# First attention of a three-layer block: the softmax weights turned by VectorE in 32x32 blocks and moved by 16 SBUF transfers per half batch, instead of transposed on TensorE

## The reference, cut to what matters

```python
x = x + xattn(layernorm(x), ctx, ctx, mask, w_q, w_k, w_v, w_o)   # 16 batches, 64 queries, 1601 keys, 16 heads of 32
x = x + attn(layernorm(x), w_qkv, ..., w_proj)                    # self-attention over 64 tokens, LoRA on q and v
x = x + ffn(layernorm(x), wg1, wg2, We, be)                       # 20 experts of 512x512, the two best per token

# xattn: the part that is changed
key, value = proj(ctx, w_k), proj(ctx, w_v)
scores = einsum('bhqd,bhkd->bhqk', query, key) / sqrt(32)
scores = where(mask == 0, -1e9, scores)
attn = softmax(scores, -1)
out = einsum('bhqk,bhkd->bhqd', attn, value)
```

## Time and profile before

| | us |
|---|---|
| median of three runs | 772.93 |
| profiled execution, first to last instruction | 772.6 |
| TensorE busy (matmul) | 708.0 |
| VectorE busy | 410.2 |
| ScalarE busy | 360.6 |
| GpSimd busy | 289.0 |

### The profile page before, as it was taken

How to read it: one execution, slowest core, us unless ns; L and a number is a source line. 1 busy time by engine, 2 the same in 40 slices (tenths; PEclk the granted TensorE clock), 3 DMA queues, 4 the chain that set the end, 5 groups by cost and what they waited for, 6 DMA issues and landing times.

```text
span 772.6 us, 16928 instructions
## 1 busy us (share of the span) xinstructions
PE 708.0 (92%) x6817; PEld 581.6 (75%) x6817; DVE 410.2 (53%) x938; ACT 360.6 (47%) x665; POOL 289.0 (37%) x259
## 2 busy tenths in 40 slices
PE   1999999999999999999999999999999766999970
PEld 0787788778878887888788977887778554788860
DVE  5834434453344424533543345735368348799965
ACT  2425445453545345535454343533455431599950
POOL 0005135513553255225532453432225132788530
PEclk9999999999999999999999999999999985799995
DMA  8401101220021101110110002021001580999818
GB/s 294 149 1 43 45 2 45 98 91 24 29 98 44 44 2 44 44 39 7 44 44 2 3 3 75 1 79 45 3 29 57 188 303 21 330 394 397 333 52 326
DMA packets 30268, 74.77 MB, mean 97 GB/s; under 512 B 4053, under 2 KB 4437, under 8 KB 29155
## 3 DMA queue, kind: packets, MB, share of 16 engines
q1 hardware_dynamic: 25778, 65.16, 23.6%
q0 software_dynamic: 4400, 8.41, 2.9%
HBM read 66.13 MB, written 13.44 MB: 103 GB/s over the span
## 4 chain that ended last, share of the span: by engine, by line
PE 86%; DVE 6%; DMA 3%; ACT 2%; issue 2%; SPq 0%; POOL 0%; DVEq 0%; POOLq 0%; ACTq 0%
PE bank L188 22%; PE bank L190 21%; PE bank L189 20%; PE bank L194 10%; PE bank L345 4%; PE bank L322 3%; DMA raw<-in_wq 2%; DVE x_sb L1611 1%; PE bank L564 1%; DMA wr<-scratch_ys 1%; PE bank L551 1%; PE bank L665 1%; PE bank L580 1%; DVE wh L1084 1%; DVE stats L1340 0%
## 5 line engine op out<-in xcount | busy, mean ns | idle before, releaser
L1637 POOL TENSOR_SCALAR pp<-pp,rl 128x400 f32<-128x400 f32 x128 | 163.8, 1297 | 234.8 <-DVE rl L1162 234.8
L1217 DVE COPY pt<-bank 128x512 f32<-128x512 f32 x64 | 44.3, 692 | 99.4 <-PE bank L194 99.3
L188 PE MATMUL bank<-chi,wk 128*128 128x400 f32 x256 | 93.5, 365 | 0.0
L844 ACT ACTIVATE pp<-pp,acc 128x400 f32<-128x400 f32 x128 | 79.0, 619 | 28.0 <-DVE acc L1250 27.7
L1250 DVE CUSTOM_DVE_ANT_0 pp<-bank,cap 128x400 f32<-128x400 f32 x128 | 66.8, 569 | 46.5 <-PE bank L322 46.5
L190 PE MATMUL bank<-chi,wk 128*128 128x400 f32 x256 | 88.3, 345 | 0.0
L189 PE MATMUL bank<-clo,wk 128*128 128x400 f32 x256 | 88.3, 345 | 0.0
L188 PE MATMUL bank<-wv,chi 128*128 128x512 f32 x200 | 83.5, 417 | 0.0
L189 PE MATMUL bank<-wv,chi 128*128 128x512 f32 x200 | 78.5, 393 | 0.0
L190 PE MATMUL bank<-wv,clo 128*128 128x512 f32 x200 | 78.5, 392 | 0.0
L761 ACT ACTIVATE pt<-bank 128x512 f32<-128x512 f32 x64 | 38.2, 597 | 76.4 <-PE bank L194 75.3
(11 more groups left out here) (238 smaller groups left out, 1387.4 us busy)
## 6 DMA issues: line engine op xcount, KB each, us to landing
wr<-in_We SPq DMA_DIRECT2D x13, 1024.0 KB, 11.6
craw<-in_ctx SPq DMA_DIRECT2D x16, 800.0 KB, 4.4
raw<-in_We SPq DMA_DIRECT2D x8, 1024.0 KB, 10.5
acc<-in_We SPq DMA_DIRECT2D x6, 1024.0 KB, 11.0
scratch_xn<-acc SPq DMA_DIRECT2D x16, 256.0 KB
wr<-scratch_ys SPq DMA_DIRECT2D x8, 512.0 KB, 7.2
x_sb<-in_x SPq DMA_DIRECT2D x2, 1024.0 KB, 8.5
out_dram<-x_sb SPq DMA_DIRECT2D x8, 256.0 KB, 5.9
```

Source lines behind the costliest of these rows:

```text
L188: pe.matmul(o, lhs[0], rhs[0], start=start, stop=False)
L844: act.activation(frame(p8), frame(p8), ACT.Exp, bias=bias, scale=-1.0, accum_out=total).then_inc(S["a_exp"], 1)
L1217: dve.tensor_copy(pt[:, p8 % 4, :, :].rearrange("p a c -> p (a c)"), at("t", 8 * (n - 1) + p8)[:, :]).then_inc(S["v_pt"], 1)
L1637: pool.tensor_scalar(frame(p8), frame(p8), rl[:, n % 2, p8:p8 + 1], None, ALU.mult).then_inc(S["g_pn"], 1)
```

## The change

The turns leave TensorE. VectorE transposes each 32x32 block of a tile in place in its grid (`turn`), into `square`, a buffer for each half of a batch that lies in the two `raw` tiles. Blocks then have to change their quarter of the partitions: `shuffle` on SyncE issues, for each half batch, 16 transfers from SBUF to SBUF, one for each pair of a source quarter and a target quarter, each of 32 partitions by 4 rows of 512 bytes (64 KB), into `pt`, which has two halves now. `pv_part` waits for all 16.

The sums of the products move to bank 3 and no longer share banks with the scores, so `s_part` no longer waits for `o_first`, and keys, values and early projections go round three banks in place of four. The lists of all engines are written anew. `wo` is loaded and split in step 0; `w2q` and `w2k` are loaded after the loop, since `square` lies in `raw`. `oh` holds two tiles in place of four.

```diff
+        turned, spreads = [banks[:, 3, 256 * j:256 * j + 256].rearrange("p (g q) -> p g q", g=4) for j in range(2)]
-        pt = sb("pt", [128, 4, 4, 128], f32, second)
+        pt = sb("pt", [128, 2, 4, 4, 128], f32, second)
+        square = [raw[:, 1 - h].rearrange("p k n -> p (k n)").rearrange("p (b x) -> p b x", b=16) for h in range(2)]
             def pv_part(n, half):
-                pe.wait_ge(S["v_pt"], 4 * n + 2 * half + 2)
-                pe.wait_ge(S["a_pt"], 4 * n + 2 * half + 2)
+                pe.wait_ge(d_sh[half], 256 * (n + 1))
...
             def cross(seg):                                  # TensorE
+                for n in range(16 * seg, 16 * seg + NB):
+                    old = n > 16 * seg
+                    values = list(range(made(n), made(n + 1)))
+                    if n:
+                        for g in range(3):
+                            k_part(n, g)
+                    s_part(n, 0)
+                    if old:
+                        pv_part(n - 1, 0)
+                    if n:
+                        k_part(n, 3)
+                    v_part(n, values[0])
+                    s_part(n, 1)
+                    if old:
+                        pv_part(n - 1, 1)
+                    for j in values[1:]:
+                        v_part(n, j)
+                last = 16 * seg + NB - 1
+                for half in range(2):
+                    if not seg:
+                        early_out(2 * half)
+                        early_out(2 * half + 1)
+                    pv_part(last, half)
...
             def cross(seg):                                  # ScalarE, per step
+                    if n:
+                        k_part(n, 0)
+                    if n + 1 < 16 * seg + NB:
+                        context(n + 1)
+                    if n:
+                        k_part(n, 2)
+                    if n == 0:
+                        act.wait_ge(S["p_q"], 8)
+                        weight_hi(wh[0], raw[:, 0], (d_raw[0], 48))
+                    exps(n, seg, 0)
+                    exps(n, seg, 1)
+                    value(n, values[0])
+                    exps(n, seg, 2)
+                    value(n, values[1])
+                    exps(n, seg, 3)
+                    for j in values[2:]:
+                        value(n, j)
...
+            def turn(n, p8):                                 # VectorE
+                half, j = divmod(p8, 4)
+                dve.wait_ge(S["g_pn"], 8 * n + p8 + 1)
+                if n and j == 0:
+                    dve.wait_ge(d_sh[half], 256 * n)
+                c = D * p8 + PW - CW * (n % 8) % 128
+                dve.transpose(square[half][:, :, 32 * j:32 * j + 32],
+                              pp[:, c:c + 512].rearrange("p (b x) -> p b x", b=16)).then_inc(S["v_pt"], 1)
...
+                for n in range(first, last + 1):
+                    old = n > first
+                    if old:
+                        for p8 in (5, 6, 7):
+                            turn(n - 1, p8)
+                    if n < last:
+                        context(n + 1)
+                    if n:
+                        k_part(n, 1)
+                    if n == 0:
+                        weight_lo(wh[0], raw[:, 0], 4)
+                    maxima(n, seg, 0)
+                    maxima(n, seg, 1)
+                    share(n, 0, seg)
+                    if n:
+                        k_part(n, 3)
+                    share(n, 1, seg)
+                    turn(n, 0)
+                    turn(n, 1)
...
+                    elif old:
+                        o_first(n - 1)
+                    maxima(n, seg, 2)
+                    maxima(n, seg, 3)
+                    share(n, 2, seg)
+                    turn(n, 2)
                     share(n, 3, seg)
+                    turn(n, 3)
+                    turn(n, 4)
...
+            def shuffle(n, half):                            # SyncE
+                sp.wait_ge(S["v_pt"], 8 * n + 4 * half + 4)
+                if n:
+                    sp.wait_ge(S["p_pv"], 2 * n - 1 + half)
+                of = square[half].rearrange("p (i a) x -> p a i x", a=4)
+                for a in range(4):
+                    for to in range(4):
+                        sp.dma_start(pt[32 * to:32 * to + 32, half, :, a, :],
+                                     of[32 * a:32 * a + 32, to]).then_inc(d_sh[half], 16)
...
+                context(first + 1, 1, chunk)
+                if seg == 0:
+                    sp.wait_ge(S["v_w"], 3)
+                    sp.dma_start(raw[:, 0], t["wo"]).then_inc(d_raw[0], 16)
+                for n in range(first, last + 1):
+                    if n > first:
+                        shuffle(n - 1, 1)
+                    if n + 2 <= last:
+                        context(n + 2, n + 2 - first, chunk)
+                    shuffle(n, 0)
+                shuffle(last, 1)
+                sp.wait_ge(d_sh[0], 256 * (last + 1))
...
+            sp.dma_start(raw[:, 1], t["w2q"]).then_inc(d_raw[1], 16)
             sp.drain().then_inc(S["s_bar"], 1)
             sp.wait_ge(S["s_bar"], BARRIER)
 
+            sp.dma_start(raw[:, 0], t["w2k"]).then_inc(d_raw[0], 16)
```

More of the change, by code:

```diff
@@ L229, in perceiver @@
         uses = [("q", m) for m in range(4)] + [("k", g) for g in range(4)] + [("q", 4 + m) for m in range(4)]
[L230 to L241, removed]
+        for n in range(16 * NC_):
+            uses += [("k", 4 * n + g) for g in range(4) if n] + [("v", j) for j in range(made(n), made(n + 1))]
+            if n == NB - 1:
+                uses += [("e", i) for i in range(EARLY)]
         use_of = {use: n for n, use in enumerate(uses)}
         def read_by(what, i):
-            if what == "t":
-                return S["a_pt" if i % 2 else "v_pt"], i // 2 + 1
             if what == "k":
@@ L252, in at, with early @@
         def at(what, i):
[L253 removed]
+            return pb[use_of[what, i] % 3]
         def freed(what, i):
             n = use_of[what, i]
[L258 removed]
+            return [read_by(*uses[n - 3])] if n >= 3 else []
+        def early(v, i):
+            return v[:, :, i % 2 * 128:(i % 2 + 1) * 128]
         def tensor(pe):
@@ L379, in redo @@
                     pe.wait_ge(S["s_redo"], REDONE + 4 * i + 2)
-                    out_product(i, oh, at("e", i)).then_inc(S["s_redo"], 1)
+                    out_product(i).then_inc(S["s_redo"], 1)
                 pe.wait_ge(S["s_redo"], REDONE + 4 * EARLY)
             def cross(seg):
[L384 to L390, removed]
-                        pv_part(n - 1, 0)
-                        for p8 in range(4, 8):
-                            t_part(n - 1, p8)
-                        early_out(2)
-                        pv_part(n - 1, 1)
[L396 to L405, removed]
@@ L415, in tensor @@
+                if seg:
+                    spread(last)
             turn_x(0)
@@ L802, in cross @@
             def cross(seg):
-                for n in range(16 * seg, 16 * seg + NB + 1):
-                    old, new = n > 16 * seg, n < 16 * seg + NB
-                    if n and not old:
+                for n in range(16 * seg, 16 * seg + NB):
+                    values = list(range(made(n), made(n + 1)))
+                    if seg and n == 16 * seg:
                         context(n)
[L807 to L818, removed]
+                    if n:
+                        k_part(n, 0)
@@ L836, in cross @@
[L836 to L849, removed]
@@ L850, in cross @@
-                    value(made(n) + 2)
-                    value(made(n) + 3)
-                    if not seg and 0 <= n - SPLIT < EARLY:
+                    exps(n, seg, 0)
[6 more added lines that the diff above has]
+                        value(n, j)
+                    if not seg and 0 <= n - SPLIT < 2:
@@ L1227, in cross @@
                     if old and seg:
-                        o_more(n - 1, b - 1)
+                        o_more(n - 1, n - 1 - first)
                     elif old:
                         o_first(n - 1)
-                    if n == NB and not seg:
-                        dve.wait_ge(S["p_o"], 4)
-                        early_add(3).then_inc(S["v_x1"], 1)
-                    if not new:
-                        break
-                    if n == 4:
-                        weight_lo(wh[0], raw[:, 0], 4)
@@ L1261, in cross @@
-                    share(n, 3, seg)
+                    maxima(n, seg, 2)
+                    maxima(n, seg, 3)
+                    share(n, 2, seg)
+                    turn(n, 2)
+                    share(n, 3, seg)
+                    turn(n, 3)
+                    turn(n, 4)
+                    if not seg and 0 <= n - 1 - SPLIT < 2:
+                        dve.wait_ge(S["a_h"], n - SPLIT)
+                        early_lo(n - 1 - SPLIT).then_inc(S["v_h"], 1)
+                for p8 in (5, 6, 7):
+                    turn(last, p8)
@@ new lines, in cross @@
+                if not seg:
```

(12 more changed lines are left out.)

152 lines of the change are left out of this document (59 added, 93 removed).

## The result

The kernel after takes 876.2 us (870.4 to 878.2, five runs) where the kernel before takes 773.0: ratio 1.131, interval 1.128 to 1.135. It is slower by 13%, outside the range that was forecast and on the other side.

The account below looks back on a forecast made before the run. TensorE's list bounded the kernel before; after, the step P is the longest of that list (21.46 us) and two loops through the transfers, 23.2 us. The sum 398.7 + 15 P gave 747 us, range 726 to 790.

Parts of the forecast that it names:

- What bounds the kernel, and what is removed: TensorE's list bounds the loop; removing four groups of transposes saves 3.6 us a step, from 25.06 to 21.46 us.
- loop B: Path through SyncE's queue that closes at pv_part(n, 1): 6.9 + 31 d + 2.3 = 23.15 us a step.
- tail: Stretch from the start of pv_part(n-1, 1) to the last turn of half 0, turn(n, 3): 6.9 us.
- landing: Time of a transfer from issue to arrival: 2.3 us, with ends 0.45 and 4.4.
- rival 3: DMA engines pace the train at 0.71 us a transfer: step 31.2 us, kernel 867 us; chance 0.09.
- Issue: Spacing of consecutive transfer issues on SyncE's queue: 0.45 us, with ends 0.36 and 0.55.
- d: Time between two consecutive issues in SyncE's queue, taken as 0.45 us; 0.01 us of it is 4.7 us of the kernel.
- Rival 2: SyncE's issue becomes the bound, slower beyond break-even 0.506 us; at 0.55 a step of 26.3, kernel 793 us; chance 0.22.
- Beginning: Step 0, from the first scores at 62.06 to pv_part(0, 0): 22.7 us.
- End: After pv_part(15, 0): 8.9 us to the last copy, then weight_lora some 4 us later, with 1.0 put in the sum.
- VectorE's turns: In-place transposes on VectorE: 0.69 us each, with ends 0.42 and 1.38; eight a step add 5.5 us.
- The three banks and the load of the context: Three banks in place of four cost nothing; the context load's 4.4 us, between SyncE's two trains, are hidden.

Follow-up runs that it names:

- experiment 4: The changed kernel with one transfer per half batch in place of 16 from the second batch on (output not right): 738.2 us, ratio 0.953 against the kernel before.
- experiment 1: A kernel without the attention, issuing only trains of 16 transfers of one shape; the shape of the change cost 0.65 us an issue on SyncE.

## Why the prediction was wrong, step by step

**What bounds the kernel, and what is removed.** Right. TensorE's own list was to fall to 21.46 us a step; experiment 4 has 21.57 on average with three value tiles, 3.6 less than before.

**The loop through SyncE.** The mechanism was right, in place and in kind: loop B, `pv_part(n, 1)` to `pv_part(n + 1, 1)` through 32 issues in one queue. Its tail was forecast at 6.9 us and is 6.73 at full clock. The landing was 2.3 and is 2.1, and doesn't grow; rival 3 (engines pace the train) is wrong.

**The step that failed** is the term *Issue*: "I take d = 0.45, with the ends 0.36 (just under the cheapest train) and 0.55 (just over the dearest)." It measured 0.674 (20.9 us for 31), outside both ends. With it B is 6.9 + 20.9 + 2.3 = 30.1 us where I had 23.15, and the sum 398.7 + 15 x 30.1 = 850 us: 104 us of the 122 between the forecast and the profiled span of 868.4. One reason is experiment 1's answer: I had written that none of the rows is a transfer inside SBUF, and then took bounds from the cheapest and the dearest of them all the same, as if size and rows were what varied. All of those I read for d were simple loads. The other is a misreading: 0.55 was not over the dearest. The same trace of before has this pair of loads in SyncE's queue, 0.60 each by the division that gave 0.39 and 0.51:

```profile
2.13 1.20 SPq L1762 DMA_DIRECT2D qc<-in_rows  x2
```

With 0.60 as the upper end B is 27.8 us and the kernel 816, still short of the result but clearly slower. Rival 2 had the mechanism, the break-even at d = 0.506 and the side; with d = 0.55 for its price, its 793 us are 83 too low.

**The remaining 18 us.** *TensorE's clock*: I had no term for it. After some of the waits `pv_part` takes 1.93 instead of 1.10 us, and keys stand 0.33 apart (280.05 to 280.38) instead of 0.18: the granted clock, 0.89 over a step, has fallen to the lower of its two levels there. Where this comes behind `pv_part(n, 1)`, it is in the tail. So it is here, one step ahead of the one shown above:

```profile
226.64 1.94 PE L332 MATMUL bank<-pt,vv 128*32 128x64 f32 x64 [2.60 <-DMA pt<-raw]
228.51 0.80 PE L191 MATMUL bank<-wv,chi 128*128 128x512 f32 x1
229.10 0.63 PE L192 MATMUL bank<-wv,chi 128*128 128x512 f32 x1
229.53 0.63 PE L193 MATMUL bank<-wv,clo 128*128 128x512 f32 x1
```

```profile
236.18 21.55 SPq L1802 DMA_DIRECT2D pt<-raw  x32
```

Products of the value tile stand 0.43 apart, not 0.23; it is 9.54 us to the first issue and 32.6 to the next `pv_part(n, 1)`, against 6.73 and 29.8 in the step behind it. Over all 15 steps the mean is 30.88, 1.1 us a step above the step at full clock, 17 in all, from which the landing and the tail, each 0.2 shorter than in the formula, take 5 back. *Beginning*: `pv_part(0, 0)` stands at 88.56, 3.8 us later than 62.06 + 22.7; 2.1 of them go to the lower clock behind TensorE's wait of 5.1 us for the maxima (granted clock 0.50 from 68.14 to 72.30), and 1.5 are its wait for the first train, which takes 3.5 us more than 16 x 0.45 and was to be hidden. *End*, 18.1 us from `pv_part(15, 0)` to `weight_lora` for 8.9 + 4.0: 10.4 in place of 7.2 to the second half's `pv_part`, the train again, and 7.7 in place of 5.7 from there, with 6.6 us of waiting for `w2q`. What follows took 2.6 less than before.

**VectorE's turns** were 0.69 by the nearest row and are 0.684. The three banks and the load of the context cost nothing visible, as forecast.

**The chances.** One hundredth of a us of d was 4.7 us of the kernel, as the text said. A quantity with that lever, measured on no row of its kind, deserved a far wider range than 0.36 to 0.55. The cheap fix was also in plain sight: the sum had one queue with 32 issues, while GpSimd was busy for 10.15 us of 25.

## What to carry over

Before a kernel moves a tile by many small transfers, count the issues per step and queue, and price each at what a transfer of just that kind costs to issue; bytes and rows come after that. If the train is longer than its cover, split it over a second queue with idle time before anything else is changed: here this alone turned 1.131 into 0.958. A bound taken from rows of another kind (loads, for copies inside SBUF) isn't a bound, and when the result hangs on it, the range must say so.

## What the runs showed of the hardware that was not expected

- An issue on SyncE cost 0.63 to 0.66 us for all shapes within SBUF and for four rows out of HBM, 16 to 256 KB; a contiguous row of 2 KB per partition out of HBM 0.46; on GpSimd 0.55, and the same in the full kernel, behind its multiplications and with VectorE at work (8.68 us for 16).
- What an issue takes also depends on what stands ahead of it in the queue. The load of the context took 0.33 us to issue in the kernel before, each of the 15 times (line 1777), with an idle queue, and 0.59 right behind a train in the kernel after (287.53); after a pause of 0.34 us it took 0.33 again (348.07). A single issue read after a pause is no price for a train.
- The Trainium skill, in "DMA: Bandwidth & Descriptors", section "Bandwidth", gives 0.95 us for a transfer of 64 KB issued from GpSimd. The trains of 64 KB here went at 0.65 us on SyncE and 0.55 on GpSimd; taken as their pace, that figure is too dear.
- ScalarE's copy of 32 partitions by 512 within SBUF takes 0.64 us, its copy of 128 partitions by 512 out of PSUM 0.60.
- TensorE's granted clock fell to its lower level behind many of the waits for the weights, and stood there for about 6 us of work (226.64 to 232.5 and 277.69 to 283.7, granted clock 0.50 in both). Behind the waits of 1.7 us and less `pv_part` always took 1.10; behind those of 2.1 to 3.2 sometimes 1.10 or 1.15, sometimes 1.6 or 1.94; behind the longer ones 1.6 to 1.94.
